# Four tiles of two batches taken one by one from path masks to query rows, with products on TensorE for the memory sums

## What is computed

```python
# layer 0: dynamic time warping of normalized tokens (56) on context rows (1500);
# each token gets the sum of the context rows on its part of the path
x = x + tanh(g_xattn[0]) * aligned_sums(layernorm(x), ctx)
# memory: 8 heads x (32 + 32) key scores, the best pair picks one of 1024 rows
sims = layernorm(x) @ folded_keys            # 448 x 512
idx, score = argmax of each half, sum of the maxima
h = gelu(layernorm(x) . w_down[idx]) * max(score, 0)
x = x + tanh(g_ffn[0]) * sum over heads(h * w_up[idx])
# layer 1
q = layernorm(x) @ Wq + bq                   # 16 heads of 8
x = x + tanh(g_xattn[1]) * (softmax(q k^T / sqrt(8)) v @ Wo + bo)
x = x + tanh(g_ffn[1]) * best_two_of_8_experts(layernorm(x))
```

## Time and profile before

| | |
|---|---|
| median of 3 runs | 517.43 us (517.33 to 517.56) |
| the profiled execution | 516.99 us, of which span 515.2 us |
| busy: PE, DVE, ACT, POOL | 422.9, 372.8, 255.2, 64.7 us |
| mean granted clock | 0.946 |
| 40 slices, clock in tenths | `9999999888999999655789999999999999999999` |

### The profile page before, as it was taken

One profiled execution on the slowest core, in us unless ns is written; L12 is line 12 of the kernel. 1 busy time (PEld: TensorE's weight loads), 2 busy tenths in 40 slices (PEclk: granted clock), 3 DMA queues, 4 the chain that ended last, 5 costly groups with the idle time before them and its releaser, 6 DMA issues.

```text
span 515.2 us, 10127 instructions
## 1 busy us (share of the span) xinstructions
PE 422.9 (82%) x4013; PEld 253.2 (49%) x4013; DVE 372.8 (72%) x979; ACT 255.2 (50%) x442; POOL 64.7 (13%) x99
## 2 busy tenths in 40 slices
PE   8998877677888888200788899999999999989996
PEld 5444433345555574000334456666666666654443
DVE  7659999997666794865686898888888884462222
ACT  4665877553322591100102456665666567655443
POOL 1000000001000001677430000210210210200000
PEclk9999999888999999655789999999999999999999
DMA  8600764334422103893162004383483582000000
GB/s 283 241 0 25 213 198 144 102 125 122 153 60 80 41 3 67 204 240 90 56 135 50 1 1 101 84 180 86 98 180 74 111 269 62 1 1 1 0 1 18
DMA packets 28941, 50.28 MB, mean 98 GB/s; under 512 B 2470, under 2 KB 18622, under 8 KB 28894
## 3 DMA queue, kind: packets, MB, share of 16 engines
q1 hardware_dynamic: 27070, 45.96, 33.0%
q0 software_dynamic: 1536, 3.67, 2.9%
q10 hardware_dynamic: 288, 0.00, 0.0%
HBM read 39.96 MB, written 9.45 MB: 96 GB/s over the span
## 4 chain that ended last, share of the span: by engine, by line
PE 47%; DVE 35%; issue 7%; POOL 6%; ACT 2%; DMA 1%; DVEq 0%
PE banks L1608 7%; PE banks L1584 7%; POOL arena L554 6%; PE banks L1639 5%; DVE arena L1213 5%; PE banks L1681 5%; DVE work L1244 5%; DVE mx L1019 4%; PE banks L1696 4%; DVE arena L1268 2%; PE banks L1452 2%; DVE work L1208 2%; DVE mx L1027 2%; PE banks L1301 2%; PE banks L1323 2%
## 5 line engine op out<-in xcount | busy, mean ns | idle before, releaser
L1019 DVE TENSOR_REDUCE mx<-banks 112x1 f32<-112x500 f32 x168 | 107.1, 675 | 16.4 <-PE banks L1584 16.4
L762 ACT ACTIVATE arena<-banks 128x896 f32<-128x896 f32 x96 | 87.9, 917 | 48.3 <-PE banks L1639 47.7
L1323 PE MATMUL banks<-steps,one 128*128 128x500 f16 (+1 forms) x188 | 53.8, 380 | 32.9 <-DVE hcol L967 32.9
L1608 PE MATMUL banks<-arena 128*32 128x112 f32 (+1 forms) x1536 | 57.1, 265 | 1.5 <-ACT arena L762 0.9
L1584 PE MATMUL banks<-ctxT,arena 96*112 96x500 bf16 x144 | 54.7, 393 | 3.8 <-DVE mx L1019 1.1
L1608 PEld LDWEIGHTS banks<-arena 128*32 128x32 f32 (+1 forms) x1536 | 33.6, 109 | 21.5 <-issue 18.9
L1244 DVE SCALAR_TENSOR_TENSOR work<-twice,banks,arena 128x202 f32<-128x202 f32 x68 | 29.5, 434 | 18.7 <-PE banks L1452 18.7
L1639 PEld LDWEIGHTS banks<-arena,ctxT 99*128 99x128 bf16 (+1 forms) x576 | 37.5, 103 | 10.2 <-issue 2.4
L1323 PEld LDWEIGHTS banks<-steps,one 128*128 128x128 f16 x188 | 19.2, 104 | 47.1 <-issue 37.4
L1639 PE MATMUL banks<-arena,ctxT 99*128 99x112 bf16 (+1 forms) x576 | 41.2, 213 | 0.3 <-issue 0.3
L640 ACT ACTIVATE arena<-banks,wts 128x375 bf16<-128x375 f32 x64 | 33.9, 597 | 7.5 <-PE banks L1370 7.5
(11 more groups left out here) (269 smaller groups left out, 697.7 us busy)
## 6 DMA issues: line engine op xcount, KB each, us to landing
ctxT<-key_parts SPq DMA_DIRECT2D x36, 375.0 KB, 6.7
key_parts<-arena SPq DMA_DIRECT2D x32, 281.2 KB, 3.1
ctxT<-in_ctx_T SPq DMA_DIRECT2D x12, 500.0 KB, 9.0
arena<-key_parts SPq DMA_DIRECT2D x12, 375.0 KB, 7.8
ctxT<-in_ctx_nat SPq DMA_DIRECT2D x5, 750.0 KB
arena<-in_ctx_nat SPq DMA_DIRECT2D x3, 750.0 KB
arena<-in_L_ffn_W SPq DMA_DIRECT2D x1, 2048.0 KB, 9.7
arena<-in_fold_w SPq DMA_DIRECT2D x1, 768.0 KB, 6.0
```

The source lines that it names most:

```text
L762: nc.scalar.activation(Pt[0:rows, g % 2, :].rearrange("p (a n) -> p a n", a=2), banks[0:rows, 2 + 2 * (g % 2):4 + 2 * (g % 2), 0:HQ // 2], ...
L1019: nc.vector.tensor_reduce(mx3[:, b % 2, u // NPIECE, u % NPIECE:u % NPIECE + 1], ps[k % 2][0:2 * NJ, 0:PIECE], AX_X, ALU.max).then_inc(s_m ...
L1323: nc.tensor.matmul(bank[:, 0:cols], one16[:, :], steps16[:, 0:cols], start=True, stop=True, skip_group_check=True)
L1608: last = nc.tensor.matmul(ps[6 + b % 2][q:q + 32, o:o + 2 * NJ], vals[0:rows, v0:v0 + 32], Pt[0:rows, g % 2, 2 * t * NJ:2 * (t + 1) * NJ], ...
```

## The change

Each tile now goes alone from its masks to its query rows.

- The 60 masks are cut in pieces (`masks(g, s0, s1)`), with alignment, normalization and choice of the tile before in between. `path_starts` on ScalarE is cut alike.
- All normalizations of the stage have 112 columns, eight instead of four. A tile lives in two PSUM banks: `ps[t]` for its scores and `ps[4 + t]` for sums, transposes, means, tokens, memory sums and queries.
- POOL makes its tables earlier, clears `picks`, and gathers tile 0 before the other tiles' sums are done. Three waits on `s_ex` guard the buffers that the gathered rows overwrite. ScalarE fills `picks`.
- `up` leaves VectorE. ScalarE makes a diagonal matrix of each head's factor (`diagonals`, eight ACTIVATEs a tile), and TensorE multiplies the gathered rows with it and accumulates over heads (`up`), which gives the sum transposed at once. VectorE only multiplies the gelu with the score (`weigh`).
- `split_queries`, `queries` and `query_rows` run by tile; ScalarE makes all copies to `QP`, two head pairs at a time.
- Batch 0's row scores come in twelve pairs (`first_scores`), reduced by twelve `first_maxima`, between the work of the later tiles. ScalarE switches between the tables of Gelu and Sqrt for each tile (`table_of`).
- The fillers of the stage are fewer: 3, 2, 12, 12, 12, 6 and 3 passes.

```diff
+    ROWS_BANK = ((0, 1, 2, 3), (5, 4, 5, 4), (6, 4, 6, 4), (7, 4, 7, 4))
...
+            def up(t):
+                pe.wait_ge(s_dg, t + 1)
+                for h in range(NHK):
+                    last = nc.tensor.matmul(ps[4 + t][:, 0:TT], gath[:, t, h, D:], diag[:, h, :],
+                                            start=(h == 0), stop=(h == NHK - 1), skip_group_check=True)
+                last.then_inc(s_oT, 1)
...
+            def diagonals(t):
+                act.wait_ge(s_hm, t + 1)
+                if t >= 1:
+                    act.wait_ge(s_oT, t)
+                for h in range(NHK):
+                    last = nc.scalar.activation(diag[:, h, :], ident[0:TT, 0:TT], ACT.Copy, scale=hcol[:, t, h:h + 1])
+                last.then_inc(s_dg, 1)
...
+                masks(3, 10, NS)
+                add_alignment(2)
+                centre(3)
+                add_alignment(3)
+                scale(3)
+                centre(4)
+                choose(2)
+                down(0)
+                scale(4)
+                weigh(0)
+                choose(3)
+                add_memory(0)
+                centre(5)
+                down(1)
+                scale(5)
+                weigh(1)
+                split_queries(0)
+                down(2)
+                add_memory(1)
+                first_maxima(0)
...
+            pool.wait_ge(s_ex, 1)
+            nc.gpsimd.memset(picks, 0.0).then_inc(s_pz, 1)
+            pool.wait_ge(s_ex, 2)
             for t in range(4):
+                if t == 1:
+                    pool.wait_ge(s_ex, 3)
                 pool.wait_ge(s_idx, t + 1)
...
-            sp.wait_ge(s_otok, 4)
+            sp.wait_ge(s_oT, 3)
             ones_rows(1, kp_words[2][NPR:NPR + 3, :])
...
+            first_scores(0)
+            mean_once(6)
+            first_scores(1)
+            variance_of(6)
+            first_scores(2)
+            up(2)
+            queries(1)
+            first_scores(3)
+            query_rows(1, 0)
+            first_scores(4)
+            mean_once(7)
+            query_rows(1, 1)
...
-            keep_busy(ps[7], 14)
             maxima_to_rows(0)
```

More of the change, by code:

```diff
@@ new lines, in _ @@
+            path_starts(NS, 2 * NS)
+            path_sums(0)
+            path_starts(2 * NS, 2 * NS + 10)
+            deviation(1)
+            path_sums(1)
+            path_starts(2 * NS + 10, 3 * NS)
+            token_rows(0)
+            act.wait_ge(s_pz, 1)
+            own = ident[:, :].rearrange("p (m r) -> p m r", r=G)
+            for c, (_, qx) in enumerate(PRODUCTS):
+                last = nc.scalar.activation(picks[:, :, qx, c::len(PRODUCTS)], own, ACT.Copy)
+            last.then_inc(s_picks, 1)
@@ L722, in _ @@
+            path_starts(3 * NS, 3 * NS + 10)
+            deviation(2)
+            path_sums(2)
+            path_starts(3 * NS + 10, 4 * NS)
+            token_rows(1)
             deviation(3)
+            path_sums(3)
+            token_rows(2)
             deviation(4)
+            table_of(4, ACT.Gelu)
+            gelu(0)
+            diagonals(0)
+            token_rows(3)
+            table_of(5, ACT.Sqrt)
+            deviation(5)
+            table_of(6, ACT.Gelu)
+            gelu(1)
@@ new lines, in _ @@
+            diagonals(1)
+            for pair in range(4):
+                query_rows(0, pair)
+            gelu(2)
+            diagonals(2)
+            table_of(7, ACT.Sqrt)
+            deviation(6)
+            query_rows(1, 0)
+            query_rows(1, 1)
+            deviation(7)
+            table_of(8, ACT.Gelu)
+            gelu(3)
+            query_rows(1, 2)
+            diagonals(3)
+            query_rows(1, 3)
+            table_of(9, ACT.Sqrt)
+            query_rows(2, 0)
+            deviation(8)
@@ L725, in maxima_rows @@
+            for pair in range(1, 4):
+                query_rows(2, pair)
+            for pair in range(4):
+                query_rows(3, pair)
             def maxima_rows(b):
@@ L782, in _ @@
             hidden(1)
-            deviation(6)
+            deviation(LN_LAST + 1)
             hidden(2)
             hidden(3)
-            nc.scalar.activation(warm[:, :], epsc[:, :], ACT.Exp)
+            nc.scalar.activation(warm[:, 3:4], epsc[:, :], ACT.Exp)
             for j in range(FC, 2 * FC):
@@ new lines, in masks @@
+            def masks(g, s0, s1):
+                for s in range(s0, s1):
+                    i = g * NS + s
+                    if s == 0 and g >= 2:
+                        ve.wait_ge(s_ex, g - 1)
+                    ve.wait_ge(s_am, i + 1)
+                    nc.vector.scalar_tensor_tensor(
+                        out=Pm[:, g % 2, s, :].rearrange("c (b j) -> c b j", j=NJ),
+                        in0=EB[:, 2 * g:2 * g + 2, s + 1:s + 1 + NJ], scalar=rowc2[:, s:s + 1],
+                        in1=Am[:, i % A_RING, :].rearrange("c (b j) -> c b j", j=NJ), op0=ALU.is_ge, op1=ALU.min
+                        ).then_inc(s_pm, 1)
@@ new lines, in query_rows @@
+            def query_rows(t, pair):
+                n0, n1 = 2 * t * TT, 2 * (t + 1) * TT
+                pe.wait_ge(s_qs, t + 1)
+                if t >= 1 and pair >= 2:
+                    pe.wait_ge(s_qpa, 4 * t + pair - 1)
+                elif t >= 2:
+                    pe.wait_ge(s_qpa, 4 * t)
+                for i in range(2):
+                    m = 2 * pair + i
+                    for x in range(3):
+                        last = nc.tensor.matmul(ps[ROWS_BANK[t][pair]][0:NPR, i * 2 * TT:(i + 1) * 2 * TT],
+                                                picks[:, m, x, :], QS[:, x, n0:n1],
+                                                start=(x == 0), stop=(x == 2))
+                last.then_inc(s_ql, 1)
@@ L1542, in _ @@
-            keep_busy(ps[5], 6)
-            for part in range(2):
-                lo, hi = LN_COLS[3 + part]
-                pe.wait_ge(s_xn, 3 + part)
-                nc.tensor.matmul(ps[2][:, lo:hi], Wq_sb, xnT[:, lo:hi], start=True, stop=True).then_inc(s_q, 1)
-            def query_rows(half, m, bank):
-                n0 = half * TOK
-                for x in range(3):
-                    last = nc.tensor.matmul(ps[bank][0:NPR, 0:TOK], picks[:, m, x, :], QS[:, x, n0:n0 + TOK],
-                                            start=(x == 0), stop=(x == 2))
-                last.then_inc(s_ql, 1)
@@ L1562, in _ @@
+            keep_busy(ps[3], 6)
+            tokens(3)
+            up(0)
+            mean_once(5)
+            variance_of(5)
+            queries(0)
+            up(1)
+            pe.wait_ge(s_picks, 1)
+            pe.wait_ge(s_idx, 4)
+            for pair in range(4):
+                query_rows(0, pair)
             pe.wait_ge(s_one[0], 16)
```

452 lines of the change are left out of this document (229 added, 223 removed).

## The result

The changed kernel takes 528.93 us (median of 4 runs, 526.61 to 531.09) where the kernel before took 517.49 on the same chip (517.33 to 517.68): a ratio of 1.0224, 95% interval 1.0184 to 1.0264. It is slower by 11.4 us; 514.2 was forecast, and 521.5 was the upper end of the range. The profiled execution is the longest of the four, 531.09 us with a span of 529.3, 14.1 above the profiled execution before (516.99).

What follows compares the result with a forecast made beforehand. POOL's gathers, then a serial chain to the loop's first score, were taken as the bound. The walk's 284.3 plus 7.4 for half clock gave 291.7, 3.2 earlier: 516.99 - 3.2 + 0.44 = 514.2 us; range 507.5 to 521.5.

Steps and rivals of the forecast that it cites:

- The bound and the gathers: POOL's 32 indirect gathers, 1.37 us each, leave the path; last rows land 11 us before VectorE asks for them.
- VectorE's work: VectorE's operations from the first mask to the last step of the split of maxima, summed to 81.4 us.
- VectorE's waits at full clock: VectorE's waits in the new order up to the split of maxima, with TensorE at full clock: 24.2 us.
- tile 3's alignment: VectorE waits while tile 3's 30 products, copy and transpose stand behind the similarity product: 4.4 us.
- the scaling of tile 2: VectorE waits 3.0 us because ScalarE makes eight diagonals and loads a table in front of its deviation.
- the pairs 8 to 10: VectorE waits 5.1 us at these score pairs, where TensorE lays a group of query rows between two pairs.
- The whole walk: New order followed through the engines from 175.28 us: loop's first score at 284.3, 10.6 us earlier, at full clock.
- The clock: TensorE falls to half clock at 219 us, returns, and is lost again at least once: 7.4 us taken.
- a price of 14.9: Upper bound of half clock's cost: the part of its 24.4 us that falls into VectorE's waits.
- the dense stretch: TensorE's work from 236 to 245 us (tile 1's products, query rows, first scores), expected to bring back full clock.
- cold clock: Rival: TensorE stays at 1.2 GHz from 219 us until the loop, first score 4.3 later, 521.5 us; chance 0.34.
- The table switches: Rival: three ScalarE table switches on the path cost beyond their loads, 518.0 us at twice 1.28 each; chance 0.03.

Runs made afterwards that it cites:

- e1: The changed kernel with filler passes of 500 columns, 192 more, put back into TensorE's waits, and one added TensorE wait: 509.81 us, ratio 0.9849.
- e12: The changed kernel, unfilled, with the loads of key rows for batches 3 to 7 cut to a corner of each: 525.10 us, ratio 1.0138.
- e0: The changed kernel run once more, unaltered, for a second trace: 525.76 us, ratio 1.0106 to the kernel before.
- e2: The changed kernel with 8 more filler passes in the one wait right ahead of the loop: 527.52 us, ratio 1.0169.
- e9: e7 with first scores from the fourth pair on and two query products ahead of products that wait for VectorE, fillers cut: 497.57 us, ratio 0.9601.
- e7: e1 with ScalarE's Exp table loaded earlier and tile 2's Sqrt table and deviation ahead of its diagonals: 506.30 us, ratio 0.9788.
- e11: e1 with up products and sums back on VectorE, one transpose a tile, no diagonals, fillers refitted: 513.69 us, ratio 0.9920.
- e8: e1 with the loads of key rows for batches 3 to 7 cut to a corner of each: 506.05 us.

## Why the prediction was wrong

**The bound and the gathers: right.** The first gather was forecast at 194.3 and came at 195.25. The last was to land at 242.3; it goes out at 243.35 and ends at 244.28, so it lands at about 246.0 (an estimate, with the prediction's 1.75). VectorE, who asks for the last tile's at 261, does not wait for it. No first score waits for key rows.

**VectorE's work: right.** 81.4 us were forecast from the first mask to the last split step, gaps included; it is busy for 77.5 in 121.0, the waits take 41.0 of the rest, and 2.5 are gaps: 80.0.

**VectorE's waits at full clock: right, 24.2 against 26.2 in e1.** By single terms: tile 3's alignment 4.4 and 4.41, the first pair 1.8 and 1.91, the scaling of tile 2 3.0 and 3.05, the gelu 1.5 and 1.46, the query split 2.5 and 2.28, the pairs 8 to 10 5.1 and 5.52. The whole walk gave the first score 10.6 earlier than before; e1 has it 9.9 earlier.

**The clock: the step that failed.** The prediction put half clock on the path at 7.4 us, half of a price of 14.9, because "the dense stretch should bring it back"; it cost 14.8. The dense stretch did bring the clock back, at 246 to 248; what was wrong is what that is worth. The clock is lost again by 252, and later returns last no longer, so two more tiles' products, most of the query rows and seven of the twelve score pairs ran at 1.2 GHz. That is the path of the rival *cold clock*, which had a chance of 0.34 and a time of 521.5, though that rival has no return of the clock at all.

That the whole price of 14.9 and the measured 14.8 agree is luck. The prediction lets the clock fall at 219; it fell at 196 and again at 210, and 3.3 us of the 14.8 come from there, a term that the prediction put at nothing. From 219 on the first trace has 11.5, not 14.9, and other executions of the same order lost up to 17.9 in all.

**What the rival's price left out.** (1) The last 24 passes of query rows, 1.9 us: the walk let them end beside VectorE's split, and at half clock they end behind it. (2) The cold start of the loop, put at 1 at most: 1.85 us in the profiled run, 2.1 in e12, and none in e0 and e2. (3) The loop itself, put at no change: 5.4 us in the profiled run, stops of TensorE and half clock behind the longest, which other executions have in part or not. So 516.99 - 9.9 + 14.8 + 1.9 + 1.85 + 5.4 = 531.0, the profiled run's 531.09.

**The table switches: the rival is out.** A switch costs its load of 1.28 us and the 0.20 of the ACTIVATE that asks for it. The Sqrt table on the path of tile 2, in ScalarE's timeline of the changed kernel:

```profile
248.99 2.34 ACT L727 ACTIVATE work<-ident,hcol 112x112 f32<-112x112 f32 x8 [1.69 <-DVE hcol L1024]
251.34 1.28 ACT L731 ACT_TABLE_LOAD   x1
252.64 0.20 ACT L731 ACTIVATE warm<-epsc 128x1 f32<-128x1 f32 x1
```

The load begins 0.01 us behind the ACTIVATEs ahead of it, and the next ACTIVATE 0.02 us behind the load. The drain of 1.38 us that the Trainium skill (ScalarE: Activation LUTs, section What ACT_TABLE_LOAD costs) counts on top is not in these rows either.

**The range** was too narrow for a kernel whose clock hangs on short waits: identical runs of the changed kernel lie between 519.9 and 531.1 us, those of the kernel before between 516.2 and 520.5. It also ended below its own rival: 517.4 + 4.3 is 521.7, and 522.7 with the cold start, not 521.5. Two smaller slips changed nothing: the half-clock terms add to 24.5, not 24.4, and 15% of the price gives 509.1, not 508.5.

## What to carry to other kernels

When a change removes fillers or cuts TensorE's work into small pieces between waits, price half clock for the whole stage, from the first thin wait on, and not for part of it: here that price (14.8 us, and 1.9 behind) turned a gain of 9.9 into a loss. Put the fillers back into the new waits first, then judge the order; and where VectorE is the bound, put a product whose inputs are ready ahead of one that waits for VectorE (8.1 us of waits in e9). Refit the fillers after each change of order: left as they were, they cost e7 some 2.5 us. The parts themselves were worth 3 to 5 us each, much less than the work that they took off VectorE (12.5 us for the up products), since most of it came back as waits for TensorE and ScalarE (26.2 us in e1, 17.7 in e11).

## What the runs showed that was not expected

TensorE stops in the loop with no wait shown, for 0.6 to 2.3 us, in every kernel whose key rows are loaded in full, the one before included (0.63 us at 348), and never where these loads are cut (e8, e12). One of 2.32 us was followed by some 7 us at 1.2 GHz and cost 5.5 us (24.89 between two splits, 19.38 without it). The Trainium skill (Runtime: NRT & Kernel Launch, section Instruction fetch mechanics) has the fetching of further instructions by DMA as mostly hidden. Most packets of the instruction queue agree: between 330 and 420 us each trace has 11 to 13 of them, and at most two in a trace have a stop behind them. But every stop of 0.3 us or more has such a packet 1.3 to 1.8 us ahead of it, and with the loads cut no stop is left, 3.8 us of e1's time are saved, and the runs of e8 lie within 0.4 us of each other.
